# The mask product of a graph network's edge rows: contraction over 128 rows in place of 1

## The chip, the cores and the metric

The kernel runs on one core of one Trainium2 chip. Times are device microseconds of one execution: 3562.28 us is the median of 3 runs of the kernel before (3558.31 to 3564.93). A changed kernel is compared with it by the same measure.

## What is computed

`x` has 100000 rows (nodes) of 128 numbers; 25000 edges lead from `src` to `dst`, sorted by `dst`, each with a weight.

```python
h = jnp.maximum(_layernorm(x, axis=-1), 0.0)
xn = _bn(x, g0, be0)
h = _bn(relu(_gcn_conv(xn, src, dst, edge_weight, W1, b1, n)), g1, be1)
h = _bn(relu(_graph_conv(h, src, dst, edge_weight, Wrel2, brel2, Wroot2, n)), g2, be2)
h = _bn(relu(_graph_conv(h, src, dst, edge_weight, Wrel3, brel3, Wroot3, n)), g3, be3)
return x + h

def _gcn_conv(x, src, dst, ew, W, b, n):
    xw = x @ W
    deg = segment_sum(ew, dst, num_segments=n) + 1.0
    dinv = rsqrt(deg)
    norm = dinv[src] * ew * dinv[dst]
    agg = segment_sum(norm[:, None] * xw[src], dst, num_segments=n)
    return agg + xw / deg[:, None] + b

def _graph_conv(x, src, dst, ew, Wrel, brel, Wroot, n):
    agg = segment_sum(ew[:, None] * x[src], dst, num_segments=n)
    return agg @ Wrel + brel + x @ Wroot
```

(The inner function calls its own input x, which is the h of the first line.) `_bn` normalizes each of 128 or 256 features over all nodes. The widths of the three layers are 128 to 256, 256 to 256 and 256 to 128.

## The kernel before

The work is done in stages with a barrier between them: a setup, the layer normalization (`norm`), the three layers (`l1`, `l2`, `l3`) and the output (`out`). In a layer two kinds of work run side by side:

- dense work: 98 tiles of 1024 nodes, as if no edge existed (most nodes have none). In layer 1 rows are loaded, transposed (L728) and multiplied by the folded weights (L716). In layers 2 and 3 a tile is loaded features first, split in two fp32r parts on ACT (L1086) and DVE (L1118), multiplied (L1059, three products for each weight block) and evicted by ACT (L1073).
- edge work: 49 chunks of 512 edges. The rows of the source nodes are gathered by POOL with indirect DMAs, turned by PE, multiplied by the edge weights, and summed along runs of edges with the same `dst` by a scan on DVE. At the last edge of each run the sum is complete, and from it and the node's own row comes the node's new row, by the edge product (`dst`: L903 in layer 1, L1283 in layers 2 and 3).

At all other edges of a run the product has to give a value that the relu turns to nothing and that never counts in the statistics. That is what the mask does: `row_neg_edge` has one bf16 number for each edge, 0 at the last edge of a run and -3.0e38 elsewhere. A chunk's 512 numbers are loaded into the tile `mk` (L846 on SP's queue in layer 1, L1398 on ACT's queue in layers 2 and 3), and a product of a row of ones with them puts the number into all 128 rows of the PSUM bank in which the edge product then accumulates: L902 in layer 1 and L1276 in layers 2 and 3, the mask product. It is run for each block of 128 output features: two for a chunk in layers 1 and 2, one in layer 3. Its operands are `ones_row`, 1 x 128 bf16, and one row of 512 bf16, so it contracts over K = 1 row. All other products of the three layers contract over 128 rows.

The order on each engine is fixed by `pipeline`: a stream of work gives its stages with lags, counted in chunks or tiles, and each engine runs through the rounds in the same order. Two dense tiles go with one chunk. PE, ACT and DVE take instructions strictly as they stand, and hold each other up by semaphores: ACT evicts what PE has multiplied, and PE waits for it before it writes a bank again.

In layer 1 the PE order around the mask product is: 8 transposes of a dense tile (L728), mask and edge product for features 0 to 127, mask and edge product for the rest, 4 transposes of edge coefficients (L881), then the dense products. In layer 2 it is 4 transposes (L1297), mask and 6 products (L1276, L1283), mask and 6 products, 4 transposes. In layer 3 it follows a dense product (L1059): mask, 4 products, then transposes (L1306).

`norm` and `out` have no mask product. In the setup POOL writes the constants and counts each on the semaphore `constants`; SP, PE and DVE wait until all `CONSTANTS` are there (L357, L400, L452).

Of the kernel before, what the change touches and what calls it, by code (L numbers as in the profile page):

```python
# [25 lines left out]
BF = mybir.dt.bfloat16  # L26
# [6 lines left out]
C = 128  # L33
# [4 lines left out]
CW = P * EG  # L38
# [3 lines left out]
ES = 2  # L42
# [63 lines left out]
def wait_use(eng, sem, i, per=1, upto=None, base=0):  # L106


    if isinstance(i, int) and i < 0:
        return  # L110
    eng.wait_ge(sem, i * per + (base + (per if upto is None else upto)))
# [42 lines left out]
def uses(slots, j, total=None):  # L154

    return len(range(j, total or units(slots), slots))
# [43 lines left out]
def build(nc, x, src, dst, ew, prm, out):  # L200
# [17 lines left out]
    def dram(name, shape, dt=FP):  # L218
        return nc.dram_tensor(name, shape, dt, kind="Internal").ap()
# [14 lines left out]
    r_neg_edge = dram("row_neg_edge", (EP,), BF)  # L234
# [13 lines left out]
    with keep:  # L248
        def sb(name, shape, dt=FP):
            return keep.enter_context(nc.sbuf_tensor(name, shape, dt))  # L250

        ident = sb("ident", [128, 128])
        ones_row = sb("ones_row", [1, 128], BF)
        w1 = sb("w1", [C, 1, H1])
        wroot = [None, None, None, sb("wroot3", [C, 2, C])]
        wrel = [None, None, sb("wrel2", [C, 2, H1]), sb("wrel3", [C, 2, C])]
# [35 lines left out]
        stood = [0] * ES  # L292


        STEPS, CONSTANTS = 27, 10
        with Phase(nc, "setup") as ph:
            wl, cst = ph.sem("weights_in"), ph.sem("constants")
            edge_in, fill = ph.sem("edges_in"), ph.sem("filled")
# [80 lines left out]
            @block.gpsimd  # L379
            def _(pool):  # L380
                pool.memset(dp_b[:, :], -1).then_inc(fill, 1)
                pool.memset(dn_b[:, :], -1).then_inc(fill, 1)
                pool.memset(rows_i[:, :, :, :], 0).then_inc(blanked, 1)
                pool.memset(rows_f[:, :, :, :], 0.0).then_inc(blanked, 1)
                pool.memset(ident[:, :], 0.0).then_inc(cst, 1)
                pool.iota(pos_i[:, :], pattern=[[1, TS]], base=0, channel_multiplier=TS).then_inc(cst, 1)
                pool.wait_ge(cst, 1)
                pool.affine_select(out=ident[:, :], in_=ident[:, :], compare_op=ALU.not_equal, fill=1.0,
                                   base=0, pattern=[[-1, 128]], channel_multiplier=1).then_inc(cst, 1)
                pool.iota(pos_t[:, :].rearrange("p (k g) -> p k g", g=EG), pattern=[[CW, EC], [1, EG]], base=0, channel_multiplier=EG).then_inc(cst, 1)  # L390
                pool.memset(ones_row[:, :], 1.0).then_inc(cst, 1)
                pool.memset(ones[:, :], 1.0).then_inc(cst, 1)
                pool.memset(zeros_c[:, :], 0.0).then_inc(cst, 1)
                pool.memset(zero_row[:, :], 0.0).then_inc(cst, 1)
                pool.memset(pad_b[:, :], 0.0).then_inc(cst, 1)
                pool.memset(pad_m[:, :], MASK).then_inc(cst, 1)
# [89 lines left out]
        by_chunk = lambda row: row.rearrange("(k o w) -> k o w", o=1, w=CW)  # L486

        def line(row, k):
            return by_chunk(row)[k].broadcast_to([C, CW])
# [136 lines left out]
        def gated(pool, table, g, per, parts):  # L626


            firsts = [pool.value_load(table[0:1, row, g:g + 1], min_val=0, max_val=most) for row, (most, _) in enumerate(parts)]  # L629
            for first, (_, slots) in zip(firsts, parts):  # L630
                for s in slots:
                    pool.wait_ge(s, first * per + per)  # L632
# [154 lines left out]
        def edge_rows(ph, ps):  # L787
# [9 lines left out]
            co_s, tu, ev, spr, msg, scn, slf, zz, mm_d, rl_d, st_d, tr, ev_t, in_s, in_m, used = (ph.slots(f"ed_{x}", ES) for x in names.split())  # L797
# [3 lines left out]
            ts, td = ph.sb("ed_src_rows", [P, ES, EG, TC]), ph.sb("ed_dst_rows", [P, ES, EG, TC])  # L801
            co = ph.sb("ed_coef", [P, ES, 2, EG])
            xs, ms, se, xd = (ph.sb(f"ed_{n}", [C, ES, CW]) for n in ("src", "message", "sum", "dst"))
            ss, mk = ph.sb("ed_same", [C, ES, CW], BF), ph.sb("ed_mask", [1, ES, CW], BF)
            ho, tb = ph.sb("ed_ho", [C, ES, 2, CW]), ph.sb("ed_rows", [P, ES, EG, C])
            zero = ph.sb("ed_zero", [C, 1])
            tiles = tab[1][0:EP, :].rearrange("(k p g) c -> k p g c", p=P, g=EG)
# [3 lines left out]
            def chunk(step, part=None):  # L811

                def at(i, j):
                    if part is None:
                        step(i, j // 2, j % 2)
                    elif j % 2 == part:
                        step(i, j // 2)

                return at
# [17 lines left out]
            def sync(sp):  # L839
                def load(i, j):  # L840
                    k = i * ES + j
                    wait_use(sp, mm_d[j], i - 1, 2)
                    wait_use(sp, scn[j], i - 1)
                    sp.sem_inc(gate_l, 1)
                    sp.dma_start(ss[:, j, :], line(r_same, k)).then_inc(in_s[j], 16)
                    sp.dma_start(mk[:, j, :], by_chunk(r_neg_edge)[k]).then_inc(in_m[j], 16)  # L846

                def store_src(i, j):
                    k = i * ES + j
                    wait_use(sp, ev[j], i, 2, 1)  # L850
                    sp.dma_start(hs[0][k][:, 0, :], xs[:, j, :]).then_inc(sto_h[j], 16)

                def store_table(i, j):
                    k = i * ES + j
                    wait_use(sp, ev_t[j], i)
                    sp.dma_start(tiles[k], tb[:, j, :, :]).then_inc(sto_t[j], 16)

                def store_dst(i, j):
                    k = i * ES + j
                    wait_use(sp, rl_d[j], i, 2)  # L860
                    sp.dma_start(hd[1][k], ho[:, j, :, :]).then_inc(sto_d[j], 16)

                def end():
                    for j in range(ES):
                        for s in (sto_h, sto_t, sto_d):
                            sp.wait_ge(s[j], 16 * uses(ES, j))

                return HALVES, [(3, chunk(load, 0)), (5, chunk(store_src, 0)), (8, chunk(store_table, 0)), (8, chunk(store_dst, 1))], end
# [257 lines left out]
        def edge_layer(ph, n, ps, slots):  # L1126
# [15 lines left out]
            in_a, in_b, in_c = ph.slots("ed_in_a", slots), ph.slots("ed_in_b", slots), ph.slots("ed_in_c", slots)  # L1142
# [7 lines left out]
            ss = ph.sb("ed_same", [C, slots, CW], BF)  # L1150
# [3 lines left out]
            xa = ph.sb("ed_xa", [C, slots, kb, CW])  # L1154
            se = ph.sb("ed_sum", [C, slots, kb, CW])
            hd_in = ph.sb("ed_hd", [C, slots, kb, CW])
            mk = ph.sb("ed_mask", [1, slots, CW], BF)
            ho_d = ph.sb("ed_ho", [C, slots, mb, CW])
            hsi = ph.sb("ed_hs", [C, slots, max(ks, 1), CW])
            zero = ph.sb("ed_zero", [C, 1])  # L1160
# [219 lines left out]
            def scalar(act):  # L1380
# [14 lines left out]
                def load_dst(i, j):  # L1395
                    k = i * slots + j
                    act.dma_start(hd_in[:, j, :, :], hd[n - 1][k]).then_inc(in_c[j], 16)
                    act.dma_start(mk[:, j, :], by_chunk(r_neg_edge)[k]).then_inc(in_c[j], 16)  # L1398

                for j in range(slots):  # L1400
                    load_source(0, j)
                    load_dst(0, j)
# [37 lines left out]
                def dst_relu(i, j):  # L1440
                    wait_use(act, sto_d[j], i - 1, 16)
                    wait_use(act, st_d[j], i - 1, mb)
                    b = bfold[n]
                    for m in range(mb):
                        wait_use(act, mm_d[j], i, mb, m + 1)
                        act.activation(ho_d[:, j, m, :], ps[:, BD + m, 0:CW], ACT.Relu, bias=b[:, m:m + 1]).then_inc(rl_d[j], 1)
                    if inside(i + 1, j):
                        load_dst(i + 1, j)
# [251 lines left out]
        with Phase(nc, "l1") as ph:  # L1700
            ps = ph.pb("ps", 8)
            edges, edges_turn = edge_rows(ph, ps)
            dense, dense_turn = dense_rows(ph, ps)
            side_by_side(ph, DI, [edges, dense, edges_turn, dense_turn],
                         last=fold(ph, 1, 2, BN, wroot[2], wfold[2], bias[2], bfold[2], ps))
        front.close()
        with Phase(nc, "l2") as ph:
            ps = ph.pb("ps", 8)
            edges, edges_ahead = edge_layer(ph, 2, ps, ES)
            side_by_side(ph, DI, [edges, dense_layer(ph, 2, 2, 2, h1, h2, ps), edges_ahead],  # L1710
                         last=fold(ph, 2, 2, BN, wroot[3], wfold[3], bias[3], bfold[3], ps))
        with Phase(nc, "l3") as ph:
            ps = ph.pb("ps", 8)
            side_by_side(ph, DI, [edge_layer(ph, 3, ps, ES), dense_layer(ph, 3, 2, 1, h2, h3, ps)],
                         last=fold(ph, 3, 1, BN, None, None, None, None))
# [25 lines left out]
```

## Time and profile before

| what | value |
|---|---|
| median of 3 runs | 3562.28 us |
| the profiled execution | 3567.39 us, its span 3565.6 us |
| PE busy | 2930.0 us, 82% of the span, 12445 products |
| PE weight loads busy | 1951.0 us, 55% |
| DVE, ACT, POOL busy | 2611.3, 2320.7 and 1332.1 us |
| HBM | 625.81 MB read, 515.28 MB written, 320 GB/s over the span |
| TensorE's mean granted clock | 0.906 |

How to read it: layer 1 is about us 390 to 1150 of the span, layer 2 about 1170 to 2270, layer 3 about 2290 to 3020, and the output the rest. PE's share over the whole span is lower than in the layers, since `norm` and `out` are bound otherwise; so a stage is read by itself. In `out` the granted clock is 0.50 (1.2 GHz) and in the steady part of the layers 1.00 (2.4 GHz). The page, slice by slice (40 of them, 89 us each; digits are tenths):

```profile
PE   3666599999996799999999999699999999554543
...
ACT  4999377777764677778787778456666666333332
...
PEclk9999799999998899999999999899999999555555
DMA  5998499999996899999999999699999999899998
```

Products are pipelined, and the end of one is modelled. So what a product costs in a stream is read from start to start, not from its own duration. PEld is the load of a product's weights, which may run while the product before it is still at work.

### The profile page before, as it was taken

The numbers are of one execution on the slowest core, as the hardware profiler recorded it, in microseconds if no ns is written. First come the engines' busy times: TensorE is split into PE (matmuls) and PEld (weight loads), VectorE is DVE, ScalarE is ACT, GpSimd is POOL, SyncE is SP. The second block draws the span as 40 slices with busy tenths as digits, with TensorE's granted clock in tenths as the row PEclk, the third lists the DMA queues.
The fourth block names the chain that finished last, engine by engine and source line by source line (L and its number), as shares of the span: only waits on it lengthen the run. The fifth ranks groups of instructions, "written<-read, shape, count | busy, mean of one in ns | idle before, by whom it ended". The sixth has DMA issues, their size and how long they took to land. (4 is left out here: it accounts for less than half of the span.)

```text
span 3565.6 us, 52119 instructions
## 1 busy us (share of the span) xinstructions
PE 2930.0 (82%) x12445; PEld 1951.0 (55%) x12445; DVE 2611.3 (73%) x5600; ACT 2320.7 (65%) x4070; POOL 1332.1 (37%) x1194
## 2 busy tenths in 40 slices
PE   3666599999996799999999999699999999554543
PEld 3665355555553567677777777455555555433432
DVE  6997488888887688888888888568777778433332
ACT  4999377777764677778787778456666666333332
POOL 1657555555551222222222220122223220266476
PEclk9999799999998899999999999899999999555555
DMA  5998499999996899999999999699999999899998
GB/s 200 346 345 301 153 331 333 332 331 333 333 331 240 266 347 341 336 336 341 340 338 342 340 338 313 207 290 344 346 346 351 346 343 321 324 367 364 382 357 238
DMA packets 344636, 1142.09 MB, mean 320 GB/s; under 512 B 55625, under 2 KB 103266, under 8 KB 294386
## 3 DMA queue, kind: packets, MB, share of 16 engines
q1 hardware_dynamic: 221468, 933.98, 69.5%
q0 software_dynamic: 62656, 77.70, 13.5%
q10 hardware_dynamic: 60438, 129.60, 10.2%
q8 instruction: 24, 0.39, 0.0%
q14 instruction: 50, 0.41, 0.0%
HBM read 625.81 MB, written 515.28 MB: 320 GB/s over the span
## 5 line engine op out<-in xcount | busy, mean ns | idle before, releaser
L1210 POOL DMA_INDIRECT l_ed_gathered<-agg_rows,pos_cols x392 | 432.5, 1103 | 1455.0 <-PE l_ps L1222 692.6
L1118 DVE TENSOR_TENSOR l_dn_hi<-l_dn_hi,l_dn_top 128x512 fp32r<-128x512 f32 x784 | 501.1, 688 | 234.5 <-ACT l_dn_top L1086 234.2
L1059 PE MATMUL l_ps<-l_dn_top,wroot_top 128*128 128x512 f32 x1176 | 503.8, 428 | 80.7 <-ACT l_dn_ho L1073 44.2
L1073 ACT ACTIVATE l_dn_ho<-l_ps,bias_fold 128x512 f32<-128x512 f32 x588 | 394.5, 681 | 156.2 <-PE l_ps L1059 155.3
L1086 ACT ACTIVATE l_dn_top<-l_dn_hi 128x512 fp32r<-128x512 f32 x784 | 447.5, 622 | 45.5 <-DMA l_dn_hi<-h_dense 45.5
L1059 PE MATMUL l_ps<-l_dn_hi,wroot_top 128*128 128x512 f32 x1176 | 466.8, 397 | 0.0
L1059 PE MATMUL l_ps<-l_dn_top,wroot_rest 128*128 128x512 f32 x1176 | 466.0, 396 | 0.0
L1648 POOL DMA_INDIRECT out<-out_rows_dst,out_cols x196 | 305.0, 1556 | 282.9 <-DMA out<-out_od_ot 182.7
L716 PE MATMUL l_ps<-l_dn_columns,w_fold 128*128 128x512 f32 x784 | 381.2, 609 | 30.5 <-ACT l_dn_ho L751 30.5
L1107 DVE BATCH_NORM_STATS2 bn_stats_all<-l_dn_ho 128x512 f32 (+1 forms) x588 | 365.7, 679 | 2.4 <-ACT l_dn_ho L1073 2.0
L1669 PE MATMUL out_ps<-ident,out_od_hi 128*128 128x128 f32 x784 | 192.8, 427 | 178.9 <-ACT out_od_hi L1657 178.9
L1059 PEld LDWEIGHTS l_ps<-l_dn_top,wroot_top 128*128 128x128 f32 x1176 | 222.6, 189 | 196.0 <-ACT l_dn_ho L1073 91.3
L605 ACT ACTIVATE norm_ln_ho<-norm_ln_x,norm_ln_nbias,norm_ln_rstd 128x128 f32<-128x128 f32 x784 | 301.7, 479 | 0.0
L617 PE MATMUL norm_ln_ps<-norm_ln_ho 128*128 128x130 f32 x1568 | 203.6, 283 | 115.5 <-ACT norm_ln_ho L605 115.5
L1685 DVE TENSOR_TENSOR out_od_ot<-out_ps,out_od_xt 128x512 f32<-128x512 f32 x196 | 135.6, 692 | 222.3 <-PE out_ps L1669 217.5
L751 ACT ACTIVATE l_dn_ho<-l_ps,bias_fold 128x512 f32<-128x512 f32 x392 | 260.1, 694 | 49.1 <-PE l_ps L716 48.8
L834 POOL DMA_INDIRECT l_ed_dst_rows<-h_rows,dst_cols x196 | 204.3, 1043 | 197.2 <-PE l_ps L916 146.8
L1669 PEld LDWEIGHTS out_ps<-ident,out_od_hi 128*128 128x128 f32 x784 | 153.8, 224 | 217.9 <-ACT out_od_hi L1657 161.4
L617 PEld LDWEIGHTS norm_ln_ps<-norm_ln_ho 128*128 128x128 f32 x1568 | 185.0, 192 | 134.2 <-ACT norm_ln_ho L605 134.0
L1657 ACT ACTIVATE out_od_hi<-out_od_hi,bn_shift,bn_scale 128x1024 f32<-128x1024 f32 x98 | 121.5, 1240 | 206.6 <-DMA out_od_hi<-h_dense 206.6
L1059 PEld LDWEIGHTS l_ps<-l_dn_hi,wroot_top 128*128 128x128 f32 x1176 | 223.2, 190 | 56.3 <-issue 12.2
L647 POOL DMA_INDIRECT h_rows<-map_values,out_cols x196 | 189.6, 967 | 169.9 <-issue 156.2
(237 smaller groups left out, 5797.5 us busy)
## 6 DMA issues: line engine op xcount, KB each, us to landing
h_dense<-l_dn_ho SPq DMA_DIRECT2D x196, 1024.0 KB, 10.8
l_dn_hi<-h_dense SPq DMA_DIRECT2D x196, 1024.0 KB, 10.4
l_dn_rows<-h_rows SPq DMA_DIRECT2D x98, 520.0 KB, 6.4
h_rows<-norm_ln_ho SPq DMA_DIRECT2D x97, 520.0 KB, 4.2
h_dst<-l_ed_ho SPq DMA_DIRECT2D x98, 512.0 KB, 10.3
l_ed_hd<-h_dst ACTq DMA_DIRECT2D x98, 512.0 KB
h_dense<-l_dn_ho SPq DMA_DIRECT2D x98, 512.0 KB, 11.6
out_od_hi<-h_dense SPq DMA_DIRECT2D x98, 512.0 KB, 15.1
```

Source lines behind the costliest of these rows:

```text
L605: ins = act.activation(ho[:, j, g, 0:C], xt[:, j, g, :], ACT.Relu, bias=nb[:, j, g:g + 1], scale=rs[:, j, g:g + 1])
L617: ins = pe.matmul(ps[:, 0, 0:TC], ho[0:rows, j, g, 0:C], ho[0:rows, j, g, :], start=first and g == 0, stop=final and g == G - 1, skip_grou ...
L716: pe.matmul(ps[:, 2 + u % 2, 0:CW], wfold[1][:, 0, m * C:(m + 1) * C], hc[:, j % 2, c * CW:(c + 1) * CW], start=True, stop=True).then_inc( ...
L751: act.activation(ho[:, j, m, c * CW:(c + 1) * CW], ps[:, 2 + u % 2, 0:CW], ACT.Relu, bias=bfold[1][:, m:m + 1]).then_inc(rl[j], 1)
L1059: ins = pe.matmul(o, a, b, start=t == 0, stop=t == len(terms) - 1)
L1073: act.activation(ho[:, j, m, c * CW:(c + 1) * CW], ps[:, u % 2, 0:CW], ACT.Relu, bias=bf[:, m:m + 1]).then_inc(rl[j], 1)
L1086: act.activation(top[:, j % 2, k, cc], hi[:, j, k, cc], ACT.Copy).then_inc(tp[j], 1)
L1107: dve.bn_stats(stats[:, m, (i * NS + j) * CH + c, :], ho[:, j, m, c * CW:(c + 1) * CW]).then_inc(st[j], 1)
L1118: dve.tensor_tensor(rest[:, j, k, cc], hi[:, j, k, cc], top[:, j % 2, k, cc].bitcast(FP), ALU.subtract).then_inc(spl[j], 1)
L1210: pool.indirect_dma_start(tg[:, j, g, :], None, tab[n - 1][:, :], bass.IndirectOffsetOnAxis(ap=pos_c[:, t:t + 1], axis=0)).then_inc(gat[j] ...
L1648: pool.indirect_dma_start(out[:, :], bass.IndirectOffsetOnAxis(ap=out_c[0:rows, t:t + 1], axis=0), rows_dst[0:rows, t, :], None, compute_o ...
L1669: ins = pe.transpose(ps[0:P, bank0 + (j % 2) * banks + b, g * C:(g + 1) * C], hi[:, j, e:e + P], ident[:, :])
```

## The change

`ones_row` becomes a full 128 x 128 array of ones. A new buffer `mask_rows` of 128 rows, two slots of 512 bf16 each, is filled with zeros once in the setup, and takes the place of the tiles `ed_mask` of all three layers. The loads write each chunk's mask into its row 0, as before into the only row. The mask product then reads 128 rows of ones and 128 rows of which 127 are zero: K = 128, the same sum. POOL has one instruction more in the setup (the fill of `mask_rows`, between `ones_row` and `ones`), and `CONSTANTS` goes from 10 to 11. The order of the other instructions is the same on every engine.

```diff
--- before.py
+++ after.py
@@ -250,7 +250,8 @@
             return keep.enter_context(nc.sbuf_tensor(name, shape, dt))
 
         ident = sb("ident", [128, 128])
-        ones_row = sb("ones_row", [1, 128], BF)
+        ones_row = sb("ones_row", [128, 128], BF)
+        mask_rows = sb("mask_rows", [128, ES, CW], BF)
         w1 = sb("w1", [C, 1, H1])
         wroot = [None, None, None, sb("wroot3", [C, 2, C])]
         wrel = [None, None, sb("wrel2", [C, 2, H1]), sb("wrel3", [C, 2, C])]
@@ -292,7 +293,7 @@
         stood = [0] * ES
 
 
-        STEPS, CONSTANTS = 27, 10
+        STEPS, CONSTANTS = 27, 11
         with Phase(nc, "setup") as ph:
             wl, cst = ph.sem("weights_in"), ph.sem("constants")
             edge_in, fill = ph.sem("edges_in"), ph.sem("filled")
@@ -389,6 +390,7 @@
                                    base=0, pattern=[[-1, 128]], channel_multiplier=1).then_inc(cst, 1)
                 pool.iota(pos_t[:, :].rearrange("p (k g) -> p k g", g=EG), pattern=[[CW, EC], [1, EG]], base=0, channel_multiplier=EG).then_inc(cst, 1)
                 pool.memset(ones_row[:, :], 1.0).then_inc(cst, 1)
+                pool.memset(mask_rows[:, :, :], 0.0).then_inc(cst, 1)
                 pool.memset(ones[:, :], 1.0).then_inc(cst, 1)
                 pool.memset(zeros_c[:, :], 0.0).then_inc(cst, 1)
                 pool.memset(zero_row[:, :], 0.0).then_inc(cst, 1)
@@ -801,7 +803,7 @@
             ts, td = ph.sb("ed_src_rows", [P, ES, EG, TC]), ph.sb("ed_dst_rows", [P, ES, EG, TC])
             co = ph.sb("ed_coef", [P, ES, 2, EG])
             xs, ms, se, xd = (ph.sb(f"ed_{n}", [C, ES, CW]) for n in ("src", "message", "sum", "dst"))
-            ss, mk = ph.sb("ed_same", [C, ES, CW], BF), ph.sb("ed_mask", [1, ES, CW], BF)
+            ss, mk = ph.sb("ed_same", [C, ES, CW], BF), mask_rows
             ho, tb = ph.sb("ed_ho", [C, ES, 2, CW]), ph.sb("ed_rows", [P, ES, EG, C])
             zero = ph.sb("ed_zero", [C, 1])
             tiles = tab[1][0:EP, :].rearrange("(k p g) c -> k p g c", p=P, g=EG)
@@ -843,7 +845,7 @@
                     wait_use(sp, scn[j], i - 1)
                     sp.sem_inc(gate_l, 1)
                     sp.dma_start(ss[:, j, :], line(r_same, k)).then_inc(in_s[j], 16)
-                    sp.dma_start(mk[:, j, :], by_chunk(r_neg_edge)[k]).then_inc(in_m[j], 16)
+                    sp.dma_start(mk[0:1, j, :], by_chunk(r_neg_edge)[k]).then_inc(in_m[j], 16)
 
                 def store_src(i, j):
                     k = i * ES + j
@@ -1154,7 +1156,7 @@
             xa = ph.sb("ed_xa", [C, slots, kb, CW])
             se = ph.sb("ed_sum", [C, slots, kb, CW])
             hd_in = ph.sb("ed_hd", [C, slots, kb, CW])
-            mk = ph.sb("ed_mask", [1, slots, CW], BF)
+            mk = mask_rows
             ho_d = ph.sb("ed_ho", [C, slots, mb, CW])
             hsi = ph.sb("ed_hs", [C, slots, max(ks, 1), CW])
             zero = ph.sb("ed_zero", [C, 1])
@@ -1395,7 +1397,7 @@
                 def load_dst(i, j):
                     k = i * slots + j
                     act.dma_start(hd_in[:, j, :, :], hd[n - 1][k]).then_inc(in_c[j], 16)
-                    act.dma_start(mk[:, j, :], by_chunk(r_neg_edge)[k]).then_inc(in_c[j], 16)
+                    act.dma_start(mk[0:1, j, :], by_chunk(r_neg_edge)[k]).then_inc(in_c[j], 16)
 
                 for j in range(slots):
                     load_source(0, j)
```

## Rows read from the trace of the kernel before

**Rows 1.** The busy table of three stretches, core 0: bounds in us, busy per engine, clock, DMA

```profile
450.00:1100.00 650.00, 621.16 (x2562) 332.55 (x2559) 544.78 (x1005) 453.87 (x749) 350.54 (x344) 1.00 0.91 331
1250.00:2200.00 950.00, 909.37 (x3871) 666.91 (x3870) 800.91 (x1206) 758.13 (x1296) 197.47 (x164) 1.00 1.00 339
2350.00:3000.00 650.00, 646.06 (x2329) 378.03 (x2327) 511.11 (x784) 433.85 (x741) 178.75 (x172) 1.00 1.00 341
```

**Rows 2.** Who waited for whom, us 450 to 1100: in total, times, longest

```profile
PE l_ps L716 <- ACT l_dn_ho L751: 28.8, 88, 0.6
```

**Rows 3.** The same view, us 1250 to 2200

```profile
PE l_ps L1059 <- ACT l_dn_ho L1073: 40.5, 49, 1.9
```

**Rows 4.** The same view, us 2350 to 3000

```profile
ACT l_dn_top L1086 <- DMA l_dn_hi<-h_dense: 1.2, 1, 1.2
```

**Rows 5.** The busy table of one stretch in the last stage

```profile
3200.00:3300.00 100.00, 49.41 (x196) 37.86 (x197) 33.21 (x48) 32.15 (x30) 68.15 (x44) 0.50 1.10 363
```

**Rows 6.** The mask tile's instructions: duration ns min/median/max, first and last start

```profile
L1276 PE MATMUL l_ps<-l_ed_mask,ones_row x147: 371/385/602, 1218.4 to 3011.3; 1*128 1x512 bf16 x147
...
L902 PE MATMUL l_ps<-l_ed_mask,ones_row x98: 384/385/385, 421.1 to 1131.3; 1*128 1x512 bf16 x98
```

**Rows 7.** The timeline of PE in layer 1: start us, us, engine, line, xcount

```profile
611.97 0.71 PE L728 MATMUL l_ps<-ident,l_dn_rows 128*128 128x128 f32 x5
612.61 0.39 PE L902 MATMUL l_ps<-l_ed_mask,ones_row 1*128 1x512 bf16 x1
612.92 1.12 PE L903 MATMUL l_ps<-l_ed_dst,w 128*128 128x512 f32 x2
613.98 0.39 PE L902 MATMUL l_ps<-l_ed_mask,ones_row 1*128 1x512 bf16 x1
...
615.26 0.60 PE L881 MATMUL l_ps<-ident,l_ed_coef 128*128 128x128 f32 x4
```

**Rows 8.** The timeline of PE's weight loads in the same stretch

```profile
612.60 0.09 PEld L902 LDWEIGHTS l_ps<-l_ed_mask,ones_row 1*128 1x128 bf16 x1 [0.17 <-issue]
...
614.83 0.14 PEld L881 LDWEIGHTS l_ps<-ident,l_ed_coef 128*128 128x128 f32 x1 [0.24 <-issue]
```

**Rows 9.** The timeline of PE in layer 3

```profile
2603.00 0.40 PE L1059 MATMUL l_ps<-l_dn_top,wroot_rest 128*128 128x512 f32 x1
2603.33 0.38 PE L1276 MATMUL l_ps<-l_ed_mask,ones_row 1*128 1x512 bf16 x1
2603.65 1.98 PE L1283 MATMUL l_ps<-l_ed_hd,wroot_fold 128*128 128x512 f32 x4
2605.47 1.88 PE L1283 MATMUL l_ps<-l_ed_sum,wrel 128*128 128x512 f32 x4
2607.18 0.60 PE L1306 MATMUL l_ps<-ident,l_ed_weight_cols 128*128 128x128 f32 x4
```

**Rows 10.** The timeline of PE in layer 2

```profile
1617.28 0.39 PE L1059 MATMUL l_ps<-l_dn_top,wroot_rest 128*128 128x512 f32 x1
1617.51 0.60 PE L1297 MATMUL l_ps<-ident,l_ed_rel 128*128 128x128 f32 x4
1618.04 0.39 PE L1276 MATMUL l_ps<-l_ed_mask,ones_row 1*128 1x512 bf16 x1
1618.36 0.50 PE L1283 MATMUL l_ps<-l_ed_hd_top,wroot_top 128*128 128x512 f32 x1
1618.69 0.40 PE L1283 MATMUL l_ps<-l_ed_hd,wroot_top 128*128 128x512 f32 x1
1618.93 0.39 PE L1283 MATMUL l_ps<-l_ed_hd_top,wroot_rest 128*128 128x512 f32 x1
```

**Rows 11.** The timeline of all engines in the setup

```profile
1.84 1.17 POOL L384 MEMSET setup_rows_f<- 98x1280 f32 x1
...
11.71 0.58 PE L402 MATMUL setup_ps<-ident,setup_prefix_all 125*1 125x125 f32 x2 [11.71 <-DVE setup_segsum L428]
```

**Rows 12.** The timeline of ACT in layer 2

```profile
1621.96 0.69 ACT L1446 ACTIVATE l_ed_ho<-l_ps,bias_fold 128x512 f32<-128x512 f32 x1 [0.20 <-PE l_ps L1283]
```


## The prediction

> **What bounds the kernel now.** I read the busy table by stage first. In the steady part of layers 1, 2 and 3 PE is busy for 621 of 650, 909 of 950 and 646 of 650 us at the full clock of 2.4 GHz (granted clock 1.00), and no other engine comes near [rows 1]. The DMA share there is 0.91, 1.00 and 1.00, so the transfers have to be ruled out before PE is called the bound. The table of waits does that: over those 650 us of layer 1 what PE waited for is an eviction on ACT, 28.8 us [rows 2], over the 950 us of layer 2 again ACT, 40.5 us [rows 3], and in layer 3 the only wait of the dense path for a load is one of 1.2 us [rows 4]. A share of 1.00 is not the ceiling either: the last stage moves 363 GB/s at a share of 1.10, where layers 2 and 3 move 339 and 341 [rows 5, 1]. So in the three layers time follows the start-to-start distance of PE's instructions, and what is saved in PE's queue should come off the span, as long as ACT keeps up.
>
> The mask product (L902, L1276) is there 98 + 147 = 245 times: twice for each of 49 edge chunks in layers 1 and 2, once in layer 3 [rows 6]. Its own busy time of 385 ns is modelled, so I leave it aside and read the starts around it.
>
> **What one mask product costs.** In layer 1 a transpose takes 0.71 - 0.60 = 0.11 us (five against four of them). From the start of five transposes to the mask's start there are 0.64 us, where 5 x 0.11 = 0.55 were due: 0.09 us lost ahead of it. The weights of the mask are not fetched ahead: PEld stands idle and then loads them at the very moment that the mask starts [rows 7, 8]. From the mask to the next product there are 0.31 us. Behind it the product with w (two instructions) stands 1.06 us before the next mask; in layer 3 the same kind of product, where nothing of K = 1 is near, takes 2607.18 - 2605.47 = 1.71 us for four instructions, 0.86 for two [rows 7, 9]. So the loss has three parts: PE drains before the mask, its weight load stands open, and the weight load of the product behind it stands open too.
>
> What would the mask product take if it ran as the full-height ones do? No row shows a full-height bf16 product. The nearest is the fp32r one over the same 512 columns, 0.24 us from start to start [rows 10]; the fp32 instruction takes 1.71 / 4 = 0.43. I take 0.23, since the columns are as many and bf16 is no wider; 0.43 is the upper end and would turn the middle part into a loss of 0.11 to 0.12 a mask.
>
> Layer 1, a chunk: 0.09 before the first mask; first mask and its product 1.37 us (612.61 to 613.98) against 0.23 + 0.86 = 1.09, so 0.28; second pair 1.28 us (613.98 to 615.26) against 1.09, so 0.19. Sum 0.56 us [rows 7].
> Layer 2, a mask: four transposes take 0.53 instead of 0.44, the mask 0.32 instead of 0.23, the first fp32r product behind it 0.33 instead of 0.24: 3 x 0.09 = 0.27, twice a chunk 0.54 us [rows 10].
> Layer 3, a chunk: 0.33 against 0.24 ahead of it, 0.32 against 0.23 for itself, and 1.82 against 1.71 for the four instructions behind: 0.09 + 0.09 + 0.11 = 0.29 us [rows 9].
> All 49 chunks: 49 x (0.56 + 0.54 + 0.29) = 49 x 1.39 = 68 us: 27 in layer 1, 26.5 in layer 2, 14 in layer 3. With 0.43 us for the mask itself it would be 68 - 245 x 0.20 = 19 us.
>
> **The parts of the change.** The ones become a 128 x 128 array and the mask row lies at partition 0 of a 128-row buffer whose other rows are zeros, so the product adds the same row. Removed: the height of one row, with the drain and the two open weight loads, if the height is what makes them. Added in the setup: one POOL memset of 128 x 1024 bf16 and one of 128 x 128 instead of 1 x 128. The nearest memset, 98 x 1280 fp32, takes 1.17 us, so I count 0.5 to 1.2 us; it lies beside the first loads, since POOL's constants are first asked for at 11.71 us by PE, which waits for DVE there [rows 11]. Cost 0; if the cover were gone, 1.2 us. The mask's transfer still brings 1 KB into one partition from the same queue, the order of every engine is the same otherwise, and no wait is added. The mask buffer is now one over all layers instead of one for each; every layer begins behind a barrier, so nothing waits for it.
>
> **What is late next.** In layer 1 ACT and DVE are busy for 70% and 84% and the evictions behind the edge products follow PE. PE's own waits for ACT there (28.8 us over 650 / 14.8 = 44 chunks, 0.65 us a chunk; 48 chunks lie between the first mask at 421.1 and the last at 1131.3, 14.8 us each [rows 6]) hang on ACT's order behind the second edge product; they move with it and stay. In layer 2 ACT is tight: it comes to the eviction of the second edge product out of a run of activations that follow each other without a wait, and waits only 0.20 us for PE there [rows 12]. When PE comes 0.54 us earlier, ACT has 0.20 there and must find the rest in the small waits behind it. I give layer 2 a loss of 2 us in all for this, and 1 us for first and last chunks, where PE waits for others anyway. Gain 65 us.
> The profiled execution took 3567.39 us, its span is 3565.6 us. So 3567.4 - 65 = 3502.4 for a profiled one; the median of the runs without a profile is 5.1 us lower (3562.28), which gives **3497 us**.
>
> **A rule that speaks against it.** The trace shows the mask's neighbours delayed by 0.09 us each. The Trainium skill, "TensorE: Matmul & The Clock Gate", section "Why this matters for your kernels", says that a single matmul with K = 32 takes as long as one with K = 128. Read alone, it would make this change worth nothing: 3562 us. It speaks of one product by itself; "TensorEngine Tiling (Array Packing)", section "Key Properties", says that changing the tiling mode drains the engine, and a drain is what the starts show. By that rule all of the stall goes, by the first none; the trace bears out the second as far as it can without a full-height bf16 product in it.
>
> **Rivals.**
> A, the forecast: height makes all three parts. For it: a change of format alone makes no gap where the trace has one, since the transposes (fp32) start 0.23 us after an fp32r product of 512 columns, as another such product does [rows 10]. 3486 to 3512 us.
> B, the number format makes the stall, not the height: bf16 between fp32 products. The mask is the only bf16 product, so the trace can't refute it. The change then does nothing: 3562 us.
> C, the transfers bound layers 2 and 3 after all (share 1.00 in both). Then only layer 1 gives its 27 us: 3535 us. Against it: PE waits for no load, and 363 GB/s are possible. It wins if more than 341 GB/s is not to be had beside PE's work.
> D, slower: B holds and the weight load grows with the height. It stands open in front of each mask; 0.09 us now, and the nearest full-height load, of a transpose, takes 0.14 [rows 8]. 245 x (0.14 - 0.09) = 12 us; were it twice the 0.09, 245 x 0.09 = 22 us: 3574 to 3584 us. It decides as soon as the load stays open and takes longer than 0.09 us. The Trainium skill's first page named above, section "LDWEIGHTS (loading the stationary operand)", holds that the load goes by columns and not by rows, which leaves D nothing; the trace has no pair of heights to test it.
> E, part of it: one of the three parts goes and the other two stay, or ACT eats most of layer 2: 3515 to 3545 us.
>
> **Chances.** A 0.62, B 0.14, C 0.09, D 0.07, E 0.08. About 0.2% (7 us) is what a measurement can tell from no change. Faster is A, C and E: 0.79; same 0.14; slower 0.07. The range runs from 3484 (A with a mask product a little shorter than 0.23) to 3550, which takes in C and E and leaves out B and D; A alone is 3486 to 3512.
>
> **What would show it.** Right: the weight load of L903/L1276's masks starts while the product before still runs; mask to next product 0.21 to 0.24 us; transposes to mask 0.11 a piece; the product behind 0.86 for two; 14.2 us instead of 14.8 a chunk in layer 1. C would show as PE waits for l_dn_hi or as DMA still at 339 to 341 GB/s with PE idle grown in layers 2 and 3. B and D: the starts as before. The forecast is wrong if the mask keeps 0.31 us, or if the gaps go and the layers still take as long.

## The result and the profile after

| | median | lowest to highest |
|---|---|---|
| before, 5 runs | 3564.93 us | 3558.31 to 3565.99 |
| the changed kernel, 5 runs | 3496.43 us | 3493.51 to 3499.50 |

The ratio is 0.9817 (95% interval 0.9803 to 0.9830): 68.5 us less. The profiled execution took 3494.98 us, its span is 3493.2 us, 72.4 us less than before. From the page the busy times of the engines, then slices as in the section on the profile before:

```profile
PE 2855.2 (82%) x12303; PEld 1958.4 (56%) x12445; DVE 2606.7 (75%) x5600; ACT 2314.4 (66%) x4070; POOL 1298.6 (37%) x1195
...
PE   3666499999996899999999998699999998445543
...
PEclk9999799999998999999999999899999999555555
DMA  5999499999996899999999998699999998999997
```

The shape is the same; layers 1 to 3 are shorter and `norm` and `out` are as they were. The busy table of the steady part of the three layers answers to [rows 1]:

```profile
450.00:1080.00 630.00, 594.04 (x2518) 339.73 (x2561) 550.12 (x1012) 456.98 (x752) 346.95 (x344) 1.00 0.94 343
1230.00:2150.00 920.00, 882.90 (x3805) 663.85 (x3846) 791.23 (x1199) 745.87 (x1288) 158.85 (x161) 1.00 1.00 348
2310.00:2930.00 620.00, 612.90 (x2218) 367.88 (x2260) 500.13 (x767) 425.51 (x727) 172.56 (x166) 1.00 1.00 349
```

PE is still at 94 to 99%, the clock still at 2.4 GHz (1.00), and the transfers run at 343, 348 and 349 GB/s where they ran at 331, 339 and 341. So the transfers didn't hold back what PE gave up. (PE's busy time reads low here: of the mask product the trace has only 103 of 245 records, as the view of its tile says; the weight loads are complete.)

The weight loads of the mask product, by lines (duration ns min/median/max, first and last start), and the one fill that was added:

```profile
L1278 PEld LDWEIGHTS l_ps<-mask_rows,ones_row x147: 95/96/146, 1187.7 to 2937.5; 128*128 128x128 bf16 x147
L904 PEld LDWEIGHTS l_ps<-mask_rows,ones_row x98: 97/98/98, 420.5 to 1102.0; 128*128 128x128 bf16 x98
...
L393 POOL MEMSET mask_rows<- x1: 941/941/941, 4.5 to 4.5; 128x1024 bf16 x1
```

From the first to the last mask product of layer 1 there are 1102.0 - 420.5 = 681.5 us, where there were 1131.3 - 421.1 = 710.2 [rows 6]: 28.7 us less. From the first of layer 2 to the last of layer 3 there are 2937.5 - 1187.7 = 1749.8 us, where there were 3011.3 - 1218.4 = 1792.9: 43.1 us less. That is 71.8 of the 72.4 us. The fill of the zeros took 0.94 us and lies at 4.5 us, far ahead of the first use of the constants [rows 11].

PE's timeline in layer 1, which answers to [rows 7]:

```profile
603.55 1.04 PE L730 MATMUL l_ps<-ident,l_dn_rows 128*128 128x128 f32 x8
604.64 1.02 PE L905 MATMUL l_ps<-l_ed_dst,w 128*128 128x512 f32 x2
605.50 0.38 PE L904 MATMUL l_ps<-mask_rows,ones_row 128*128 128x512 bf16 x1
605.72 1.02 PE L905 MATMUL l_ps<-l_ed_dst,w 128*128 128x512 f32 x2
```

and the weight loads of the same stretch, which answer to [rows 8]:

```profile
604.32 0.10 PEld L904 LDWEIGHTS l_ps<-mask_rows,ones_row 128*128 128x128 bf16 x1
604.43 0.41 PEld L905 LDWEIGHTS l_ps<-l_ed_dst,w 128*128 128x128 f32 x2
605.08 0.10 PEld L904 LDWEIGHTS l_ps<-mask_rows,ones_row 128*128 128x128 bf16 x1 [0.24 <-issue]
605.50 0.41 PEld L905 LDWEIGHTS l_ps<-l_ed_dst,w 128*128 128x128 f32 x2 [0.33 <-issue]
```

Each of the three parts of the loss (PE drained ahead of the mask, the mask's weight load in the open, the next product's weight load in the open) is gone. The mask's weights are loaded at 604.32, while the transposes still run; the second mask's at 605.08, 0.42 us ahead of its product at 605.50. The first mask product's own record is one of those missing, but there is no room for doubt: from the eight transposes to the product with w there are 604.64 - 603.55 = 1.09 us, 8 x 0.11 and 0.21 for the mask. The product with w takes 605.50 - 604.64 = 0.86 us (1.06 before), the mask 605.72 - 605.50 = 0.22 (0.31 before), and its product again 0.86 (the next transposes start at 606.58).

Layer 3, which answers to [rows 9]:

```profile
2609.46 0.39 PE L1061 MATMUL l_ps<-l_dn_top,wroot_rest 128*128 128x512 f32 x1
2609.91 1.88 PE L1285 MATMUL l_ps<-l_ed_hd,wroot_fold 128*128 128x512 f32 x4
2611.63 1.88 PE L1285 MATMUL l_ps<-l_ed_sum,wrel 128*128 128x512 f32 x4
2613.35 0.60 PE L1308 MATMUL l_ps<-ident,l_ed_weight_cols 128*128 128x128 f32 x4
```

From the last dense product to the edge product there are 0.45 us, 0.23 of it the dense product's and 0.22 the mask's, where there were 0.65; the four instructions behind take 1.72 us instead of 1.82. Together 0.30 us a chunk.

Layer 2, which answers to [rows 10]:

```profile
1618.02 0.40 PE L1285 MATMUL l_ps<-l_ed_hd_top,wroot_rest 128*128 128x512 f32 x1
1618.25 0.39 PE L1278 MATMUL l_ps<-mask_rows,ones_row 128*128 128x512 bf16 x1
...
1618.71 0.40 PE L1285 MATMUL l_ps<-l_ed_hd,wroot_top 128*128 128x512 f32 x1
...
1619.64 0.40 PE L1285 MATMUL l_ps<-l_ed_hd_top,wroot_rest 128*128 128x512 f32 x1
1619.94 0.66 PE L1299 MATMUL l_ps<-ident,l_ed_rel 128*128 128x128 f32 x4
1620.43 0.60 PE L1224 MATMUL l_ps<-ident,l_ed_gathered 128*128 128x128 f32 x4
```

The second mask product starts 0.23 us behind the product before it (0.33 before the change), and from it to the second product behind it there are 0.46 us (0.65 before): 0.29 us a mask, 0.6 a chunk. What is new is further down: from the last product (1619.64) to the transposes (1619.94) there are 0.30 us instead of 0.23, and the four transposes take 0.49 instead of 0.43. The table of waits for us 1230 to 2150 says what they wait for (engine, line, what it waited for: us in total, times, longest):

```profile
PE l_ps L1061 <- ACT l_dn_ho L1075: 36.7, 42, 1.6
...
PEld l_ps L1299 <- ACT l_ed_rows L1437: 14.4, 43, 0.3
```

The second line was not there before: L1299's transposes wait for ACT's eviction of the turned rows (L1437), which holds their weight loads up by 0.33 us a chunk, of which 0.13 show on PE. The first line is the old wait for ACT [rows 3], 36.7 us over 43 chunks where it was 40.5 over 44. For layer 3 the one line on loads reads, beside [rows 4]:

```profile
ACT l_dn_top L1088 <- DMA l_dn_hi<-h_dense: 4.2, 3, 2.1
```

3 waits and 4.2 us over 620 us instead of one and 1.2 over 650: still next to nothing.

Chunk by chunk, from the start of one instruction to its start in the next chunk, the median went from 14.76 to 14.17 us in layer 1 (-0.59), from 21.95 to 21.50 in layer 2 (-0.45) and from 14.75 to 14.49 in layer 3 (-0.26).

### The profile page after: what moved, and what is told of

It reads as the page before. It is cut to its first block and busy times, and to the rows that moved or that the text cites. A ratio compares the mean times of both kernels' runs of the same rounds, so it can differ in the third digit from the quotient of the medians.

```text
span 3493.2 us, 51978 instructions
## 1 busy us (share of the span) xinstructions
PE 2855.2 (82%) x12303; PEld 1958.4 (56%) x12445; DVE 2606.7 (75%) x5600; ACT 2314.4 (66%) x4070; POOL 1298.6 (37%) x1195
## 5 line engine op out<-in xcount | busy, mean ns | idle before, releaser
L1212 POOL DMA_INDIRECT l_ed_gathered<-agg_rows,pos_cols x392 | 400.2, 1021 | 1441.5 <-PE l_ps L1224 713.5
L1061 PE MATMUL l_ps<-l_dn_top,wroot_top 128*128 128x512 f32 x1176 | 500.4, 425 | 76.8 <-ACT l_dn_ho L1075 39.8
L1061 PE MATMUL l_ps<-l_dn_top,wroot_rest 128*128 128x512 f32 x1176 | 468.8, 399 | 0.0
L1061 PE MATMUL l_ps<-l_dn_hi,wroot_top 128*128 128x512 f32 x1176 | 466.6, 397 | 0.0
L1061 PEld LDWEIGHTS l_ps<-l_dn_top,wroot_top 128*128 128x128 f32 x1176 | 222.7, 189 | 189.2 <-ACT l_dn_ho L1075 83.1
L1061 PEld LDWEIGHTS l_ps<-l_dn_hi,wroot_top 128*128 128x128 f32 x1176 | 223.4, 190 | 58.8 <-issue 12.0
```

The lines of the kernel that those rows point to most:

```text
L1061: ins = pe.matmul(o, a, b, start=t == 0, stop=t == len(terms) - 1)
L1212: pool.indirect_dma_start(tg[:, j, g, :], None, tab[n - 1][:, :], bass.IndirectOffsetOnAxis(ap=pos_c[:, t:t + 1], axis=0)).then_inc(gat[j] ...
```

## Experiments

The runs were made in three sets, each on a chip of its own. The first chip behaves as the one of the prediction. On the second and third, which are alike, the stage `norm` takes some 112 us longer (the first mask product of layer 1 is at 533 instead of 421 us), so totals are compared by their ratio to the kernel before on the same chip, and layers by their chunks. What `norm` looks like there is told at the end.

### How high the product has to be

```diff
-pe.matmul(o, ones_row[:, :], mk[:, j, :], ...)
+pe.matmul(o, ones_row[0:64, :], mk[0:64, j, :], ...)     # k64; 0:65 in k65, 0:32 in k32
```

k64: 

> The changed kernel, with the mask product over the first 64 of the 128 rows. Theory 'mode' (the array is switched to a form with fewer rows for a product of up to 64 rows, and the switch drains it and leaves two weight loads open): K = 64 stalls as K = 1 does, 3564 us, mask to next product 0.31 us. Rival 'height' (the stall shrinks with the rows left out): about half of the gain, 3530 us. Rival 'one row is special': as the changed kernel, 3496 us.

k65: 

> The same with 65 rows. Theory 'mode': 65 rows need the full array, no switch, 3496 us and mask to next product 0.22 us. Rival 'height': like 64 rows, 3530 us.

k32: 

> The changed kernel with the mask product over 32 rows. Theory 'mode': as K = 1, 3564 us, mask to next product 0.31 us. Rival 'height': a quarter of the gain, 3547 us.

Measured: k64 0.9999 (0.9990 to 1.0009) of the kernel before, k65 0.9826 (0.9810 to 0.9842), k32 3672.1 us in its one run, where the kernel before took 3681.4 on that chip; with one run its chunks say more than its total. Chunks: 14.76, 21.97 and 14.77 us with 64 rows; 14.18, 21.51 and 14.48 with 65; 14.76, 21.95 and 14.76 with 32. PE's timeline in layer 1 with 64 rows:

```profile
656.35 1.04 PE L730 MATMUL l_ps<-ident,l_dn_rows 128*128 128x128 f32 x8
657.32 0.39 PE L904 MATMUL l_ps<-mask_rows,ones_row 64*128 64x512 bf16 x1
657.64 1.12 PE L905 MATMUL l_ps<-l_ed_dst,w 128*128 128x512 f32 x2
658.70 0.39 PE L904 MATMUL l_ps<-mask_rows,ones_row 64*128 64x512 bf16 x1
...
657.32 0.09 PEld L904 LDWEIGHTS l_ps<-mask_rows,ones_row 64*128 64x128 bf16 x1 [0.17 <-issue]
```

and with 65:

```profile
662.68 1.04 PE L730 MATMUL l_ps<-ident,l_dn_rows 128*128 128x128 f32 x8
663.56 0.38 PE L904 MATMUL l_ps<-mask_rows,ones_row 65*128 65x512 bf16 x1
663.78 1.02 PE L905 MATMUL l_ps<-l_ed_dst,w 128*128 128x512 f32 x2
664.64 0.38 PE L904 MATMUL l_ps<-mask_rows,ones_row 65*128 65x512 bf16 x1
...
663.45 0.10 PEld L904 LDWEIGHTS l_ps<-mask_rows,ones_row 65*128 65x128 bf16 x1
```

With 64 rows there are 0.97 us from the transposes to the mask, 0.32 for the mask and 1.06 for the product behind it; with 65 rows 0.88, 0.22 and 0.86. The mask's weight load (the last line of each, from the view of the weight loads) starts together with the 64-row mask, and 0.11 us ahead of the 65-row one. One row more brings the whole gain. So it is not K = 1 that is dear, and the stall doesn't shrink with the rows left out: it is there with 1, 32 and 64 rows and gone with 65 and 128. The Trainium skill, "TensorEngine Tiling (Array Packing)", section "Tiling Modes", knows row tilings of 32, 64 and 128 rows, and its section "Key Properties" says that a change of mode drains the engine; the step between 64 and 65 agrees. No line of a trace names the mode, so what the runs show is the step in the starts and in the weight loads, and the mode is the explanation that fits it. (That 32 and 64 rows cost the same shows that the two smaller forms are equal in this.)

### Does every short product pay, or the change of form?

```diff
 pe.matmul(o, ones_row[:, :], mk[:, j, :], start=True, stop=False)
+pe.matmul(o, ones_row[:, :], mk[:, j, :], start=False, stop=False)   # MASK halved
```

before_twice: 

> The kernel before with each mask product (K = 1) issued twice in a row, each adding half of the mask. Theory 'mode': the second is in the mode already and its weights load ahead, so it costs its 512 columns alone, 0.22 us: 245 x 0.22 = 53 us, 3617 us. Rival 'each short product pays': 0.22 + 0.30 us each, 127 us, 3691 us.

Measured: 1.0164 (1.0147 to 1.0181), 58 us more; chunks 15.19, 22.39 and 14.97 us: 0.43, 0.44 and 0.22 more, which is 0.22 for each product added. PE's timeline in layer 1:

```profile
651.06 0.39 PE L902 MATMUL l_ps<-l_ed_mask,ones_row 1*128 1x512 bf16 x1
651.28 0.37 PE L903 MATMUL l_ps<-l_ed_mask,ones_row 1*128 1x512 bf16 x1
651.59 1.12 PE L904 MATMUL l_ps<-l_ed_dst,w 128*128 128x512 f32 x2
```

The second short product starts 0.22 us behind the first and doesn't stall, and the 0.31 us now stand behind the last of the two. So the price hangs on the change of form (from a product over 128 rows to one over 64 or fewer, and back), not on the product.

```diff
+wait_use(pe, rl_d[j1], i1, 2, 1)
+wait_use(pe, ev_t[j], i)
+for m in range(2):
+    pe.matmul(ps[:, (SECOND, FIRST)[m], 0:CW], ones_row[:, :], mk[:, j, :], start=True, stop=False)
 for m in range(2):
     o = ps[:, (SECOND, FIRST)[m], 0:CW]
-    pe.matmul(o, ones_row[:, :], mk[:, j, :], start=True, stop=False)
     pe.matmul(o, w1[...], xd[:, j, :], start=False, stop=True).then_inc(mm_d[j], 1)
```

pair_l1: 

> The kernel before, K = 1, with the two mask products of a chunk in layer 1 one behind the other, ahead of both edge products. Theory 'mode': one switch a chunk instead of two, 49 x 0.30 = 15 us less, 3549 us. Rival 'each short product pays': no change, 3564 us.

Measured: 0.9971 (0.9958 to 0.9985), 11 us less on a chip where the kernel before takes 3681 us. A chunk of layer 1 took 14.46 us instead of 14.76: the 0.30 us forecast, with K = 1 as before.

```profile
751.08 1.04 PE L728 MATMUL l_ps<-ident,l_dn_rows 128*128 128x128 f32 x8
752.05 0.60 PE L899 MATMUL l_ps<-l_ed_mask,ones_row 1*128 1x512 bf16 x2
752.58 1.98 PE L902 MATMUL l_ps<-l_ed_dst,w 128*128 128x512 f32 x4
```

Transposes to masks 0.97 us, the two masks together 0.53 (0.22 and 0.31), then four instructions in one go. One change of form a chunk instead of two.

### What bounds the layers now

after_twice, the same edit of the changed kernel: 

> The changed kernel with each mask product issued twice in a row, each adding half of the mask. If PE bounds all three layers: 245 x 0.216 = 53 us more, 3549 us. If the transfers bound layers 2 and 3: only layer 1's 98 x 0.216 = 21 us more, 3518 us. If ACT had taken over layer 2 altogether: its 21 us are missing, 3528 us.

Measured: 0.9959 (0.9945 to 0.9973), so 0.0142 of 3563 us, 51 us, more than the changed kernel. Chunks 14.60, 21.82 and 14.70: 0.43, 0.32 and 0.21 more. Work added to PE shows in full in layers 1 and 3; in layer 2 0.11 us of 0.43 vanish, in the wait for ACT that the change had brought (L1299's wait for L1437 stands in no line of after_twice's table). The transfers bound none of the three layers.

no_mask and no_mask_b drop the mask products from the changed kernel, and with them the masking of all edges but the last of a run:

```diff
-pe.matmul(o, ones_row[:, :], mk[:, j, :], ...)
-pe.matmul(o, w1[...], xd[:, j, :], start=False, stop=True)
+pe.matmul(o, w1[...], xd[:, j, :], start=True, stop=True)
```

no_mask: 

> The changed kernel without any mask product (the mask is still loaded; the values at the other edges of a run are not masked). If PE bounds all three layers still: 245 x 0.216 = 53 us less than the changed kernel, 3443 us. If ACT bounds layer 2 since the change: 32 us less, 3464 us. If the transfers bound layers 2 and 3: 21 us less, 3475 us.

no_mask_b: 

> The changed kernel without mask products, again, beside the changed kernel. If PE bounds layers 1 and 3 and not layer 2: 49 x (0.43 + 0.24) = 33 us less than after_again; with the delay of layer 2 (0.23 us a chunk) 22 us less; if PE bounds layer 2 as well: 53 us less.

Measured: 0.9771 (0.9753 to 0.9788) and 0.9789 (0.9774 to 0.9805), on the second and third chip; after_again, below, is 0.9833 on the third. That is 17 us less there (3599.98 against 3617.24), where PE's queue got 53 us shorter. Chunks: 13.74, 21.73 and 14.25 us against 14.17, 21.74 and 14.49. Layer 3 gives 0.24 a chunk and is bound by PE still. Layer 2 gives nothing chunk by chunk. In no_mask's table of waits for 700 us of layer 2 the wait of the transposes for ACT's L1437 (L1297 and L1435 in this kernel) has come through to PE itself:

```profile
PE l_ps L1297 <- ACT l_ed_rows L1435: 11.2, 33, 0.4
```

That is 0.34 of the 0.43 us that PE's queue got shorter by: what ACT does ahead of that eviction bounds layer 2 now. (From its first to its last chunk layer 2 is 8 us shorter in no_mask_b than in after_again all the same. All of it lies in the first chunk, 15.3 us against 23.5, and no run tells why.) Layer 1 gives 0.43 in most chunks, but in three of them the chunk takes 19 to 22 us, so that from the first to the last only 3 us are left of 21. POOL's timeline in no_mask_b shows what comes ahead of the first of them:

```profile
674.29 1.22 POOL L836 DMA_INDIRECT l_ed_src_rows<-h_rows,src_cols  x1 [4.71 <-issue]
```

Before one gather POOL stands for 4.71 us and waits for nothing that the trace shows. Such a pause comes every 112 gathers of layer 1, in each kernel profiled (in the changed kernel at 562, 760 and 958 us, 5.4 to 5.8 us from one gather's start to the next). Beside the 0.3 us between two gathers POOL is idle for 4.3 us a chunk in the kernel before, 3.8 in the changed one and 2.7 in no_mask_b. On the first chip that takes the pause in; on the third three chunks of the changed kernel take 14.9 to 16.3 us; and with a chunk of 13.7 us PE stood idle for 4.3, 5.2 and 4.4 us at one place behind each pause. The steps from the gather to PE's stop were not followed one by one, so that the pause is the cause is argued from its place and size.

### Where 0.15 us a chunk of layer 2 went

```diff
 def load_dst(i, j):
     act.dma_start(hd_in[:, j, :, :], hd[n - 1][k]).then_inc(in_c[j], 16)
-    act.dma_start(mk[0:1, j, :], by_chunk(r_neg_edge)[k]).then_inc(in_c[j], 16)
 ...
 def store_dst(i, j):                                  # SP
     sp.dma_start(hd[n][i * slots + j], ho_d[:, j, :, :]).then_inc(sto_d[j], 16)
+    load_mask(i + 1, j)                               # the same load, on in_m[j]
```

mask_on_sp: 

> The changed kernel, but in layers 2 and 3 the mask row's load is issued by SP behind the chunk's store, and not by ACT (0.32 to 0.45 us of ACT a chunk). Theory 'ACT took 0.15 us a chunk of layer 2' (the chunk went from 21.95 to 21.50 us where 0.60 was due): it comes back, 7 us, 3489 us. Rival 'something else took it': 3496 us.

Measured: 0.9836 (0.9823 to 0.9850), and layer 2 took 21.74 us a chunk. That is more than the changed kernel's 21.50 and the opposite of what I expected. As no_mask had 21.73 too, the chip came under suspicion, and both were run again beside the changed kernel.

after_again: 

> The changed kernel once more, on the same chip as the next three. In layer 2 the runs no_mask and mask_on_sp took 21.73 and 21.74 us a chunk, where the changed kernel took 21.50: ACT came 0.5 us late to the first eviction of the dense tiles in some 30 of 36 chunks. If that belongs to those kernels, this one takes 21.50 again and 0.982 of the kernel before. If it belongs to the chip they ran on, it may take 21.7 here too.

mask_on_sp_b: 

> The mask row's load on SP's queue in layers 2 and 3, again, beside the changed kernel. If the delay belongs to the kernel: 21.74 us a chunk in layer 2, 11 us more than after_again in all. If to the chip: as after_again or up to 7 us less.

Measured: after_again 0.9833 (0.9818 to 0.9848), 21.74 us a chunk; mask_on_sp_b 0.9855 (0.9839 to 0.9870), 21.74. The first chip gave 21.51 (k65), so the 0.24 us come with the second and third chip and not with these edits, and moving the load brings nothing: the wait for L1437's eviction is 10.7 us in 700 in mask_on_sp_b and in after_again alike, so the DMA issue on ACT was not what delays it. On the third chip the change of this study is worth 62 us of 3679, where it was 68.5 of 3565. ACT in layer 2, in the changed kernel's first profile and on the third chip (after_again):

```profile
1711.84 1.06 ACT L1430 ACTIVATE l_ed_rel<-l_ps 128x512 f32<-128x512 f32 x2
1713.08 0.69 ACT L1075 ACTIVATE l_dn_ho<-l_ps,bias_fold 128x512 f32<-128x512 f32 x1 [0.17 <-PE l_ps L1061]
```

```profile
1746.30 1.09 ACT L1430 ACTIVATE l_ed_rel<-l_ps 128x512 f32<-128x512 f32 x2
1748.06 1.47 ACT L1075 ACTIVATE l_dn_ho<-l_ps,bias_fold 128x512 f32<-128x512 f32 x2 [0.67 <-PE l_ps L1061]
```

The eviction behind L1430 starts 1.24 us behind that pair's start on the one and 1.76 on the other. ACT is not busy meanwhile: it stands idle for 0.17 and 0.67 us and waits for PE's product (L1061). The last instruction of that product starts at 1712.56 and at 1747.01, the same 0.7 us behind the pair. But its semaphore update, by which ACT learns of it, stands in the trace 0.41 us behind its start on the one and 0.95 on the other. So it is the signal of PE's product that comes half a microsecond late, and not ACT.

Of 36 chunks in the middle of layer 2 the first eviction starts over 0.8 us behind its product (0.52 is usual) in 25 in after_again, in 32 in mask_on_sp, and in none in the changed kernel's first profile or in k65. A chunk with it takes 21.77 us in after_again and one without it 21.51, which is the first chip's figure: that is the whole 0.24. It is not the chip alone: in k32 and pair_l1, on the second chip too, no signal is late in these chunks, and a chunk takes 21.95 as on the first, and all six runs without a short product on these two chips have it, in 11 to 31 of the 36 chunks. Why is open. In the kernel before the eviction comes late in 7 chunks, but there the signal is on time and ACT itself is late; these chunks and the ones behind them cost 4.5 us.

```diff
-stages = [(l_rel, sum_top), (l_dst, table_out(0))] if n < 3 else []     # ACT
+stages = [(l_dst, table_out(0)), (l_rel, sum_top)] if n < 3 else []
```

table_first: 

> The changed kernel with two stages of ACT exchanged in layer 2: the eviction of the turned rows (L1437, for which PE waits 0.33 us a chunk in the table of waits) ahead of the fp32r part of the sums. Theory 'ACT took 0.15 us a chunk of layer 2': PE's wait goes, 21.36 us a chunk, 7 us less than after_again. Rival 'the wait only moves to the sums' product': no change.

Measured: 0.9806 (0.9792 to 0.9819), 3607.28 us where after_again took 3617.24 on the same chip: 10 us less. (Its ratio is the lowest of the kernels that do all the work, though it is within the intervals of the changed kernel's 0.9817 on the first chip.) Layer 2 took 21.39 us a chunk. The wait of PE for L1437 in after_again, 700 us of layer 2:

```profile
PEld l_ps L1299 <- ACT l_ed_rows L1437: 10.7, 32, 0.3
```

is not in table_first's table at all. In its place stands a wait of DVE (L1368) for the activation that was moved back, 33 times and 9.1 us in all, and no wait of PE for DVE came with it.

Not all of the 10 us are the order's: of the 36 chunks 12 have the late eviction here and 25 in after_again. The two can be told apart by reading chunks with and without it by themselves. Without it a chunk takes 21.39 us in table_first and 21.51 in after_again, with it 21.64 and 21.77: 0.12 to 0.13 us less in both groups, which is what the wait for L1437 had cost PE. Over 49 chunks the order is worth 6 us. The 13 late evictions fewer, at 0.25 us each, are another 3, and whether the new order made them fewer or they vary by themselves, this one pair doesn't tell.

## Why the prediction was right, point by point

- The time: 3497 us forecast, 3496.43 measured; 65 us forecast, 68.5 measured between the medians and 72.4 between the profiled executions. That the forecast hit to 0.6 us is luck in part: the gain was 3.5 us too small, and the kernel before, from which it was taken off, has its median at 3564.93 over five runs, 2.7 us above the 3562.28 of the three that I had. The two nearly cancel.
- That PE bounds the three layers, and that a share of DMA of 1.00 is no ceiling: right. The transfers rose to 343 to 349 GB/s and the one wait for loads in layer 3 stayed at 4.2 us in 620 (rival C fell), and after_twice put 0.43 us a chunk back into layer 1 for two products of 0.22 and 0.21 into layer 3 for one.
- The three parts of the stall, 0.56, 0.54 and 0.29 us a chunk: all three went, 0.59 in layer 1, 0.26 to 0.30 in layer 3. Over 49 chunks the sum was 1.5 us short in layer 1, since I took 0.23 us for the mask product itself, which takes 0.22, and the rows are rounded to 0.01.
- That the number format is not the cause: rival B and with it D fell, by k64 against k65. The format is the same there, and the height differs by one row. The weight load of 128 rows takes 0.096 to 0.098 us, of one row 0.091; it wouldn't have mattered even in the open.
- Layer 2: the mechanism was right and its size was off, with luck in the sum. I expected 0.54 less 0.04 a chunk for ACT; it was 0.60 less 0.15, 7 us lost and not 2. ACT's lateness struck at L1299, which waits for L1437, not at the eviction of the edge product that the prediction watched [rows 12]. Against that stood 6 us that I had not seen: from the first to the last chunk layer 2 got 28 us shorter, where 49 x 0.45 are 22. Of these 4.5 are seen: in the kernel before ACT came late to a dense eviction in 7 of 36 chunks, up to 1.1 us each, and in the changed kernel in none. That is a figure of one execution; in k64, k32 and pair_l1, which stall as the kernel before does, it is 3 or 4 chunks.
- The fill in the setup: hidden, 0.94 us.
- The rule that the prediction set against itself, that a product over few rows takes as long as one over 128: it holds for the product's own columns (0.22 us for one row in before_twice, 0.22 for 128 rows after the change), and not for what the product does to its neighbours.
- What the prediction did not tell: that 64 rows would be no better than one. It called the number of rows "height" and had no row on how much of it is wanted.

## What to carry to other kernels

In this kernel a product over 1, 32 or 64 rows in a stream of full-height products costs some 0.3 us beside its columns on PE: 0.1 us drained ahead of it and two weight loads that nothing hides. (Tried with bf16 and 512 columns between fp32 and fp32r products; a short fp32 product was not.) It is paid for each change of form and not for each product, so either fill the operands with zeros up to more than 64 rows or put the short products side by side. Read it in the starts of the neighbours and in where the weight load lies; the product's own busy time (385 ns before, 379 after) says nothing.

When the bound engine gets shorter, look at which engine comes to the meeting points without slack. In layer 2 the next 0.12 us a chunk lay in the order of two activations, and making PE shorter still gave nothing there.

## What the runs showed of the hardware that was not expected

- 64 and 32 rows stall as one row does (a chunk of layer 1 takes 14.76 us with each), and 65 rows not at all (14.18).
- On the second and third chip the semaphore update of one product a chunk of layer 2 came 0.95 instead of 0.41 us behind its start, in 25 of 36 chunks of the changed kernel and in none of k32 and pair_l1.
- POOL stood still for 4 to 6 us every 112 indirect DMAs in layer 1, in every kernel, waiting for nothing in the trace.
- The chips differ in `norm`: 3563 us for the kernel before on the first, 3681 and 3679 on the second and third. The busy table for us 150 to 250 of the changed kernel in its first profile and on the third chip:

```profile
150.00:250.00 100.00, 66.47 (x518) 60.13 (x517) 91.28 (x586) 100.00 (x261) 61.52 (x64) 1.00 0.99 344
```

```profile
150.00:250.00 100.00, 55.71 (x355) 50.21 (x354) 60.92 (x384) 68.89 (x178) 49.22 (x51) 0.81 0.69 234
```

344 against 234 GB/s, and a granted clock of 0.81 of full speed, that is 2.4 GHz for part of the stretch and 1.2 GHz for the rest; all engines are less busy there. Which of these comes first the rows don't tell. The same kernel in layer 1 takes 14.17 us a chunk on both. Why `norm` is slower there was not tried.
